# Where the deviations of the query heads are taken: on GpSimd by a power, or on ScalarE by a logarithm and an exponential that VectorE refines

## The reference

```python
def _ln(t, w, b):
    m = jnp.mean(t, axis=-1, keepdims=True)
    v = jnp.var(t, axis=-1, keepdims=True)
    return (t - m) * jax.lax.rsqrt(v + EPS) * w + b
...
q = _ln((x @ Wq + bq).reshape(b, s1, H, HD), qn_w, qn_b)
k = _ln(kv[..., :HD], kn_w, kn_b)
ctx = _attn(qT, k.transpose(0, 2, 1, 3), v.transpose(0, 2, 1, 3))
```

## Time and profile before

| what | before |
|---|---|
| three executions | 972.93, 978.85, 978.91 us |
| the profiled execution's own time | 978.07 us |
| its span, first to last instruction | 976.3 us |
| PE busy | 892.5 us, 91% of the span |
| DVE busy | 675.8 us, 69% |
| POOL busy | 481.4 us, 49% |
| ACT busy | 449.3 us, 46% |
| mean granted TensorE clock | 0.984 of full speed |

### The profile page before, as it was taken

How to read it: one execution, slowest core, us unless ns; L and a number is a source line. 1 busy time by engine, 2 the same in 40 slices (tenths; PEclk the granted TensorE clock), 3 DMA queues, 4 the chain that set the end, 5 groups by cost and what they waited for, 6 DMA issues and landing times.

```text
span 976.3 us, 19636 instructions
## 1 busy us (share of the span) xinstructions
PE 892.5 (91%) x7569; PEld 509.7 (52%) x7569; DVE 675.8 (69%) x1313; ACT 449.3 (46%) x748; POOL 481.4 (49%) x558
## 2 busy tenths in 40 slices
PE   1677999999999999999999898899989999999996
PEld 0444666666666666666666554444434444444442
DVE  6967887788877888788887749665543454445862
ACT  3445556665576655666566634222322332332210
POOL 1457777887778877788772420110720010004833
PEclk9889999999999999999999999999999999999998
DMA  7613000000000000000022026222453244236683
GB/s 269 187 54 134 9 17 19 6 18 18 15 18 3 18 17 17 18 3 18 15 68 90 12 68 256 87 87 90 127 147 113 87 163 138 86 102 210 193 248 109
DMA packets 42415, 81.90 MB, mean 84 GB/s; under 512 B 11778, under 2 KB 12098, under 8 KB 42370
## 3 DMA queue, kind: packets, MB, share of 16 engines
q1 hardware_dynamic: 37378, 66.58, 20.6%
q0 software_dynamic: 4992, 14.70, 5.4%
HBM read 67.62 MB, written 13.65 MB: 83 GB/s over the span
## 4 chain that ended last, share of the span: by engine, by line
PE 44%; POOL 29%; DVE 11%; issue 9%; ACT 3%; DMA 3%; POOLq 1%; SPq 1%; DVEq 0%; ACTq 0%
PE ps L1181 13%; PE ps L1183 13%; PE ps L1182 13%; POOL hrs L665 11%; POOL pr L721 4%; POOL y_fetched L817 3%; PE ps L1187 3%; POOL rstd L652 2%; POOL dk L681 1%; POOL gate L691 1%; POOL od L697 1%; PE ps L1353 1%; DMA y_fetched<-y_scratch,idx_get 1%; POOL kraw L703 1%; POOL pr L723 1%
## 5 line engine op out<-in xcount | busy, mean ns | idle before, releaser
L1154 ACT ACTIVATE big<-ps 128x512 f32<-128x512 f32 x64 | 38.2, 597 | 231.3 <-PE ps L1183 217.6
L665 POOL TENSOR_TENSOR hrs<-hve,neg_half 128x16 f32<-128x16 f32 x43 | 131.9, 3067 | 3.4
L2213 DVE TENSOR_SCALAR big<-big 128x512 f16<-128x512 f32 x64 | 27.9, 435 | 113.6 <-ACT big L1154 100.6
L1181 PE MATMUL ps<-w2h,big 128*128 128x512 f16 x256 | 97.7, 382 | 3.3 <-DVE big L1692 3.3
L1181 PE MATMUL ps<-big,w1h 128*128 128x512 f16 x256 | 97.0, 379 | 0.8 <-DVE big L1692 0.8
L1182 PE MATMUL ps<-w2l,big 128*128 128x512 f16 x256 | 97.5, 381 | 0.0
L1183 PE MATMUL ps<-w2h,big 128*128 128x512 f16 x256 | 97.5, 381 | 0.0
L1182 PE MATMUL ps<-big,w1h 128*128 128x512 f16 x256 | 97.0, 379 | 0.0
L1183 PE MATMUL ps<-big,w1l 128*128 128x512 f16 x256 | 97.0, 379 | 0.0
L817 POOL DMA_INDIRECT y_fetched<-y_scratch,idx_get x32 | 39.3, 1228 | 96.8 <-DMA y_scratch<-big 87.4
L800 POOL DMA_INDIRECT big<-x_scratch,token_of x16 | 17.2, 1076 | 141.0 <-PE ps L1187 82.0
(11 more groups left out here) (342 smaller groups left out, 2398.8 us busy)
## 6 DMA issues: line engine op xcount, KB each, us to landing
wst<-in_w SPq DMA_DIRECT2D x28, 1024.0 KB
x_scratch<-xn SPq DMA_DIRECT2D x16, 256.0 KB, 2.1
y_fetched<-in_w SPq DMA_DIRECT2D x4, 1024.0 KB, 14.7
out<-x_all SPq DMA_DIRECT2D x4, 1024.0 KB
pr<-in_w_attn SPq DMA_DIRECT2D x3, 1024.0 KB, 8.3
x_all<-in_w_attn SPq DMA_DIRECT2D x3, 1024.0 KB, 11.8
x_all<-in_x SPq DMA_DIRECT2D x1, 3072.0 KB, 12.7
y_scratch<-big SPq DMA_DIRECT2D x12, 256.0 KB
```

The source lines that it names most:

```text
L665: pool.tensor_tensor(hrs[n][:, :], hve[n][:, :], neg_half[:, :], ALU.pow).then_inc(hdev[n], 1)
L1154: act.activation(hg[f % 2], psum[f % 2][:, 512:1024], ACT.Gelu, scale=UN).then_inc(hg_r, 1)
L1181: nc.tensor.matmul(o, lh, rh, start=first, stop=False)
```

## The change

The head deviation of the queries leaves POOL in the steps. ACT takes it with a logarithm and an exponential, placed in its list right behind `x_hi` and ahead of `o_out`. DVE sharpens it with a Newton step in three parts that are spread between pieces that it had: behind the scaled keys, behind `gf`, behind `xtl`. The scaled queries then come ahead of the gate's floor. The semaphore `hdev[2]` counts five for a sequence instead of two. In the drain the same three parts run one behind another as before. Keys and linear attention keep their deviations on POOL.

```diff
+        HDEV = (2, 2, 5)
...
@@ POOL body
                 on(s[2], head_deviation, 1)
-                on(s[2], head_deviation, 2)
                 on(s[2], out_bias)
...
@@ ACT
+            def head_deviation(s, n):
+                after(act, hv[n], s[0])
+                act.activation(hln[n][:, :], hvar[n][:, :], ACT.Ln, bias=eps_head[:, n, 0:1]).then_inc(hdev[n], 1)
+                after(act, hdev[n], s[0], nth=1, per=HDEV[n])
+                act.activation(hrs[n][:, :], hln[n][:, :], ACT.Exp, scale=-0.5).then_inc(hdev[n], 1)
...
                 on(s[0], x_hi)
+                on(s[2], head_deviation, 2)
                 on(s[1], o_out)
...
@@ DVE
             def head_norm(s, n, dst, src, done, scale=1.0):
-                after(dve, hdev[n], s[0], nth=2, per=2)
+                after(dve, hdev[n], s[0], nth=HDEV[n], per=HDEV[n])
...
+            def refine_q(s, part):
+                after(dve, hdev[2], s[0], nth=2 + part, per=HDEV[2])
+                if part == 0:
+                    ins = dve.scalar_tensor_tensor(newton[2][:, :], hvar[2][:, :], DV * EPS_HEAD[2], hrs[2][:, :], ALU.add, ALU.mult)
+                elif part == 1:
+                    ins = dve.scalar_tensor_tensor(newton[2][:, :], newton[2][:, :], -0.5, hrs[2][:, :], ALU.mult, ALU.mult)
+                else:
+                    ins = dve.scalar_tensor_tensor(hrs[2][:, :], newton[2][:, :], 1.5, hrs[2][:, :], ALU.add, ALU.mult)
+                ins.then_inc(hdev[2], 1)
...
                 on(s[2], b1_k_norm)
+                on(s[2], refine_q, 0)
                 on(s[1], a1_gate)
+                on(s[2], refine_q, 1)
                 on(s[0], a1_low)
+                on(s[2], refine_q, 2)
+                on(s[2], b1_q_norm)
                 on(s[1], a1_gate_floor)
-                on(s[2], b1_q_norm)
                 on(s[3], b2_low)
```

More of the change, by code:

```diff
@@ L1047, in body @@
                 on(s[1], x2_hi)
[L1049 to L1053, removed]
             def drain(p, q, r):
@@ L1960, in refined @@
             def refined(s, n):
+                if n == 2:
+                    for part in range(3):
+                        refine_q(s, part)
+                    return
                 after(dve, hdev[n], s[0], nth=2, per=2)
```

## The result

The changed kernel took 994.73 us in the median of four runs (993.6 to 995.39). The kernel before took 976.35 in the median of the four runs beside it. The ratio is estimated at 1.02, with a 95% interval of 1.0173 to 1.0227 (the two medians alone give 1.019). So the change makes the kernel slower, clear of the noise; whether by more or by less than 2% the interval leaves open. The prediction had 975.5 us and a range of 970.5 to 981: the result lies outside, on the slow side.

A forecast was written before the change was run, and what follows sets the result against it. PE was taken as the bound, busy 29.83 of 31 us a step. 978.07 - 1.7 (steps 3 to 15) - 1.2 (step 2) = 975.2 us, 976.0 against the median; forecast 975.5, range 970.5 to 981.

The forecast's parts named there:

- POOL: On POOL: 14 powers of 3.24 us removed, some 50 us of busy time, worth nothing as such.
- DVE, the refinement: On DVE behind `kraw`: three small instructions priced 0.10, 0.10 and 0.20 us; `qraw` starts 1.27 us earlier, `xtl` 0.20 later.
- Rival 3: Slower by a new wait behind `xtl`, through PE and ACT: 980 us; chance 14% small form, 4% large.
- the free 0.33: Slip of `xtl` at which the gain of 0.13 us a step is used up; beyond it, time is lost.
- step 2: Step without a fourth stage, where PE waits 1.36 us before the turn of `qraw`: gain of 1.2 us.
- the slip of `xtl`: On DVE: `xtl` starts 0.20 us later behind two new instructions; bounds 0.35 and 0.55.
- The 13 steps: Steps 3 to 15: PE's scores 0.13 us earlier in each, 1.7 us in all.
- rival 4: ACT's logarithm waits for `hvar`, so `qraw` comes no earlier than POOL gave it: 978 us, chance 3%.
- Rival 2: The queries come early and nobody uses it; steady steps give nothing, step 2 alone gains: 977 us, chance 23%.
- Rival 1: POOL is the bound, so each step loses PE's 1.17 us of waiting, 16.4 in all: 962 us, chance 6%.

The follow-up runs named there:

- e2: The kernel before with POOL's addition (`out_bias`) put ahead of the queries' deviation, no new instruction: 995.32 us, 1.0219 of the kernel before.
- e1: The changed kernel with POOL's addition (`out_bias`) moved behind the bias of the values: 970.95 us, 0.9967 of the kernel before.
- e7: The kernel before with only POOL's addition moved behind the bias of the values: 973.64 us, 1.0003 of the kernel before.
- e4: The changed kernel with POOL's addition in its place but cut into two instructions of 256 columns: 991.72 us, 1.0166.
- e3b: The changed kernel with POOL's addition moved away and a one-tile POOL multiplication of 128x512 in its old place: 979.77 us, one execution.

## Why the prediction was wrong

**The step that failed** is the one called *POOL*. It priced the removal as "Worth nothing as such: the next thing on which POOL is waited for is the deviation of `od`". I asked who waits for POOL's pieces, and overlooked that `out_bias`, for which nobody waits, moves 3.5 us forward as well against `kraw` (from 3.45 behind its start to 0.06 ahead of it), and what it then runs beside. The step *DVE, the refinement* carried this on: it let `kraw` take 0.62 to the next start. It took 1.68. None of my four rivals contained it. Rival 3 was on the right side but named another place, `xtl`; it needed a slip of 1.1 us for more than 1% (by its own prices it is 1.16: 9.8 and the 1.0 of step 2, over 13 steps, on top of the free 0.33), and `xtl` did slip by 1.22 behind `kraw`'s start, 1.05 of it for a reason that isn't in it.

**The sign behind it in the profile** was there, twice. The power of the queries took 3.24 us and that of `od` 2.91: the former started beside `kraw`. I used the 3.24 as a price and did not ask why two equal instructions differ by 0.3. The trace of e2 bears it out as the same contention seen from POOL's side: there the power of the queries starts after `kraw` has ended and takes 2.92 in every step, and it is the addition of the epsilon, now beside `kraw`, that is longer by 0.46.

The second sign is in the drain of the kernel before, where the Newton parts ran already. I took their price from the middle one, 0.175 us. Its neighbours, with the same 16 columns, and what POOL did at their longest:

```profile
L1962 DVE SCALAR_TENSOR_TENSOR newton<-hvar,hrs x5: 110/167/1180, 516.4 to 547.4; 128x16 f32<-128x16 f32 x5
...
L1964 DVE SCALAR_TENSOR_TENSOR hrs<-newton,hrs x5: 174/174/1545, 516.8 to 548.8; 128x16 f32<-128x16 f32 x5
```

```profile
543.55 1.71 POOL L721 TENSOR_TENSOR pr<-pr,rc 128x896 f32<-128x896 f32 x1 [1.38 <-DVE rc L1907]
...
543.74 1.54 DVE L1964 SCALAR_TENSOR_TENSOR hrs<-newton,hrs 128x16 f32<-128x16 f32 x1
...
547.26 1.27 POOL L709 TENSOR_TENSOR vx<-vx,bkv_sb 128x512 f32<-128x512 f32 x1
547.39 1.18 DVE L1962 SCALAR_TENSOR_TENSOR newton<-hvar,hrs 128x16 f32<-128x16 f32 x1 [0.62 <-ACT hrs L1053]
```

Each began less than 0.2 us behind a POOL instruction that reads two SBUF tiles and ended within 0.05 us of its end. A minimum, a median and a maximum that are this far apart ask what the long one ran beside.

**The clock.** I had it as 1.1 us in step 2 that a clock that stays up would give back. It fell in six more steps instead and cost 8.8 us, and I priced no wait of PE by what it does to the clock. In step 2 itself it fell in every trace here: its mean between 81 and 112 us is 0.94 before and in e1, and 0.89 in the changed kernel.

**What was right**, shown by e1, where the collision is away. `qraw` starts 2.18 us after `kraw` (the text had 2.2, before 3.51), `xtl` 1.38 (1.4). The scores come 5.55 after `kraw` against 5.78, 0.23 earlier instead of 0.13, and steps are 0.23 shorter; that the slip of `xtl` was 0.15 and not 0.20 makes up a part of the difference. The time is 3.2 us under before (the sum had 2.9), but that the two are so near is in part luck. The 13 steps gave 3.0 instead of 1.7. Step 2 was to give 1.2, and the way from its `kraw` to the next is only 0.57 shorter in the trace of e1: the turn of `qraw`, which was to be free of its wait of 1.36, waited 0.89, now for ACT's `kT`, a wait that the prediction did not have. From step 3 on ACT did not wait for `hvar` and DVE did not wait for the exponential (in step 2 ACT waited 0.27), so rival 4 is out. Rival 2 is out by e1 and e7: somebody uses the early queries. Rival 1, POOL as the bound, is out: e1 leaves POOL a wait of 5.7 us before the deviation of `od` and gains 3, where the rival had 16. The Newton parts show 0.16 to 0.17 each but delay their follower by about 0.08, so the overlap of neighbours was the right reading and the fixed price per small instruction was not paid in full here.

## What to carry to other kernels

When an engine's list gets shorter, write down what the pieces behind the removed one will now run beside, above all those that nobody waits for. For each new pair of POOL and DVE, look at where the operands lie: in this kernel a DVE instruction with two operands in SBUF went from 0.70 to 1.75 us beside a POOL addition of two SBUF tiles, and one with an operand in PSUM stayed at 0.69. Moving the piece for which nobody waits into a gap turned a loss of 2% into a gain of 0.3%, and of 0.8% with the keys treated alike.

## What was not expected of the hardware

- POOL's memset of 128x512 does not touch such a DVE instruction (0.69), a multiplication that reads one tile adds 0.41 us to it, an addition that reads two adds 1.05.
- The two engines alternate instruction by instruction: two halves of POOL's work held up two DVE instructions, the second of only 16 columns (0.70 against 0.16 us), and POOL's second half took 1.18 us against 0.73 for the first.
- Idling of PE that grew from 0.4 or 0.5 to 1.4 or 1.6 us before one turn let the granted clock fall to 0.50 of full speed, in six of 14 steps, and each fall cost 1.4 to 1.5 us. The length of the idling alone does not tell where it falls. With two waits of 0.9 to 1.0 and 0.8 (e4) it fell in four steps, with 1.4 or 1.6 and mostly another 0.35 (e2) in three, at 0.9 to 1.1 us each, and with 0.7 to 0.9 and 0.3 (e3b) in none. Before the turn of the keys two waits alternate; the falls came with the longer one (1.6) in the changed kernel and in e2, and with the shorter one (0.9) in e4. Why in these steps is open.
- One execution of the kernel before lost some 4 us at the start of the second expert, 2.7 of it as idling of PE. Its first runs spread from 972.9 to 978.9, which may have the same reason. Its cause is open; nothing was tried on it.
